# A Perceiver block on one core: Gelu by way of tanh and a polynomial on GpSimd, the temperature MLP spread over three pairs of steps, second scores without a pause

## The reference

```python
scores = qk / math.sqrt(dk)
mean_sim = scores.mean(axis=(-2, -1))
max_sim = scores.max(axis=-1).mean(axis=-1)
probs = jax.nn.softmax(scores, axis=-1)
entropy_proxy = jnp.var(probs, axis=-1, ddof=1).mean(axis=-1)
feats = jnp.stack([mean_sim, max_sim, entropy_proxy], axis=-1)
hidden = jax.nn.gelu(_linear(feats, w1, b1), approximate=False)
hidden = jax.nn.gelu(_linear(hidden, w2, b2), approximate=False)
log_t = jnp.clip(_linear(hidden, w3, b3), LOG_T_MIN, LOG_T_MAX)
t = jnp.exp(log_t)[..., None]
attn = jax.nn.softmax(qk / (2.0 * t), axis=-1)
```

## Time and profile before

| | |
|---|---|
| median of 3 executions | 1214.36 us (1212.34 to 1218.31) |
| profiled execution | span 1213.1 us; its total is not given apart from the span |
| TensorE busy | 1101.5 us (91%) |
| VectorE busy | 812.4 us (67%) |
| ScalarE busy | 765.5 us (63%) |
| GpSimd busy | 406.0 us (33%) |
| mean granted clock of TensorE | 0.897 of 2.4 GHz |
| table loads on ScalarE | 33, 1.283 us each |

### The profile page before, as it was taken

The page is one execution under the profiler, slowest core; times in us unless marked ns, Lnnn a source line. Parts: engine busy times, 40 slices in busy tenths (PEclk is TensorE's granted clock), DMA queues, the critical chain, the costliest instruction groups (busy, mean ns, idle before and its releaser), DMA issues.

```text
span 1213.1 us, 39205 instructions
## 1 busy us (share of the span) xinstructions
PE 1101.5 (91%) x14964; PEld 892.8 (74%) x14964; DVE 812.4 (67%) x2128; ACT 765.5 (63%) x1547; POOL 406.0 (33%) x420
## 2 busy tenths in 40 slices
PE   3867799999999999999999999999999999999864
PEld 3535587878888787878878797878787887867743
DVE  4467667566776776677777776577667777578245
ACT  2434576776766676767766776667767676766521
POOL 2268352223232331433232332333143233331223
PEclk9968798987979897989999898989889898989787
DMA  4610010201010111102010111102020100000000
GB/s 132 193 29 27 23 37 4 61 11 42 19 44 21 36 29 28 37 2 54 11 45 20 37 29 29 36 4 61 2 54 11 45 20 19 3 2 6 8 2 9
DMA packets 46812, 38.85 MB, mean 32 GB/s; under 512 B 14576, under 2 KB 46000, under 8 KB 46640
## 3 DMA queue, kind: packets, MB, share of 16 engines
q1 hardware_dynamic: 46640, 36.41, 11.1%
HBM read 34.30 MB, written 2.10 MB: 30 GB/s over the span
## 4 chain that ended last, share of the span: by engine, by line
PE 75%; DVE 12%; issue 5%; ACT 4%; DMA 2%; POOL 1%; SPq 1%; DVEq 0%; ACTq 0%; POOLq 0%
PE pjp L665 14%; PE s1p L704 14%; PE s2p L735 13%; PE pjp L658 12%; PE pvp L752 8%; DVE est L1392 3%; DVE negm L1386 2%; PE tlp L848 2%; PE tlp L866 1%; PE tlp L787 1%; ACT ering L1045 1%; PE tlp L842 1%; PE s2p L725 1%; PE s2p L645 1%; PE tlp L809 1%
## 5 line engine op out<-in xcount | busy, mean ns | idle before, releaser
L1386 DVE TENSOR_REDUCE negm<-s1p 128x1 f32<-128x400 f32 (+1 forms) x512 | 289.8, 566 | 199.1 <-PE s1p L704 196.6
L1045 ACT ACTIVATE ering<-s1p,negm 128x400 f32<-128x400 f32 (+1 forms) x512 | 303.8, 597 | 118.6 <-DVE negm L1386 112.2
L1056 ACT ACTIVATE pring<-s2p 128x512 f32<-128x512 f32 x427 | 240.8, 565 | 148.1 <-PE s2p L735 145.1
L704 PE MATMUL s1p<-kt,qbd 32*128 32x400 f32 (+1 forms) x1024 | 305.2, 608 | 28.1 <-ACT ering L1045 26.1
L1392 DVE BATCH_NORM_STATS2 est<-ering 128x6 f32<-128x400 f32 (+1 forms) x512 | 290.7, 568 | 19.6 <-ACT ering L1045 19.6
L735 PE MATMUL s2p<-q2bd,kt 32*128 32x128 f32 (+1 forms) x3192 | 244.6, 285 | 0.0
L735 PEld LDWEIGHTS s2p<-q2bd,kt 32*128 32x128 f32 (+1 forms) x3192 | 233.3, 194 | 5.8
L658 PE MATMUL pjp<-cr,wkv 128*128 128x256 f32 (+1 forms) x1344 | 192.4, 295 | 29.7 <-DVE vt L1358 19.2
L1264 POOL TENSOR_TENSOR cr<-stage,cr 128x512 fp32r<-128x512 f32 (+1 forms) x112 | 132.1, 1180 | 234.3 <-ACT cr L1036 234.3
L658 PEld LDWEIGHTS pjp<-cr,wkv 128*128 128x128 f32 x1344 | 171.8, 198 | 45.5 <-issue 29.1
L665 PE MATMUL pjp<-wkv,cr 128*128 128x256 f32 (+1 forms) x1200 | 195.7, 318 | 10.0 <-ACT kt L1018 9.8
(11 more groups left out here) (278 smaller groups left out, 1033.1 us busy)
## 6 DMA issues: line engine op xcount, KB each, us to landing
stage<-in_ctx SPq DMA_DIRECT2D x96, 256.0 KB, 3.0
qbd<-q_dram SPq DMA_DIRECT2D x128, 8.0 KB, 1.8
stage<-in_ctx SPq DMA_DIRECT2D x16, 65.0 KB, 2.5
vt<-in_x SPq DMA_DIRECT2D x1, 1024.0 KB, 6.8
...
```

The source lines that it names most:

```text
L704: nc.tensor.matmul(s1p[u % 3][:, 0:w], qbd[s.par][rows, g, :], kt[s.par][rows, g, lo:lo + w], start=True, stop=True).then_inc(s1_full, 1)
L1045: nc.scalar.activation(ering[:, u % 3, 0:w], s1p[u % 3][:, 0:w], ACT.Exp, bias=negm[s.par][:, p, c:c + 1]).then_inc(s1_exp, 1)
L1056: nc.scalar.activation(ring_place(s, v)[0:m, 0:n], s2_bank(s, v)[0:m, 0:n], ACT.Exp).then_inc(s2_exp, 1)
L1386: nc.vector.tensor_reduce(negm[s.par][:, p, ch:ch + 1], s1p[u % 3][:, 0:w], AX.X, ALU.max, negate=True).then_inc(s1_max, 1)
```

## The change

The Gelu is no longer a ScalarE function. ScalarE computes x/2 and x squared from the matmul's output (`gelu_in`). GpSimd raises a polynomial in x squared to an argument for tanh, in ten operations on 16 or 64 columns, each of which waits for the one before by semaphore. ScalarE computes the tanh (`gelu_tanh`), which is in the table of exp, and GpSimd finishes with two operations. The weights of the MLP are widened with zeros to 128 rows and columns. The three MLP matmuls go to steps 5, 7 and 9, the first ahead of its step's projection and the others behind theirs. Second scores have no pause, projections and context splits move, the last part of the hidden rows' quantization moves from position 68 to 66 (step 4 to 2), and finishing a batch's output from steps 14 and 15 to 12 and 13.

```diff
-PJ_PLAN = [(1, ("k", 4, 0)), (3, ("v", 4, 0)), (5, ("k", 5, 0)), (9, ("v", 5, 0)), (11, ("k", 6, 0)),
-           (12, ("v", 6, 0)), (13, ("m",)), (17, ("k", 0, 1)), (19, ("v", 0, 1)), (21, ("k", 1, 1)), (23, ("v", 1, 1)),
+PJ_PLAN = [(1, ("k", 4, 0)), (3, ("v", 4, 0)), (5, ("k", 5, 0)), (7, ("v", 5, 0)), (9, ("k", 6, 0)),
+           (11, ("v", 6, 0)), (13, ("m",)), (17, ("k", 0, 1)), (19, ("v", 0, 1)), (21, ("k", 1, 1)), (23, ("v", 1, 1)),
...
-CTX_AT = {1: (5, 0), 9: (6, 0), 11: (0, 1), 15: (1, 1), 20: (2, 1), 24: (3, 1), 28: (4, 1)}
+CTX_AT = {1: (5, 0), 4: (6, 0), 11: (0, 1), 15: (1, 1), 20: (2, 1), 24: (3, 1), 28: (4, 1)}
-S2_IDLE = (38, 39)
-S2_AT = [s for s in range(14, 14 + S2U + 2) if s not in S2_IDLE]
-S2_EARLY = S2_AT.index(STEPS + 5)
-STATS_AT = [1, 3, 8, 10]
-MLP_AT = {5: 0, 6: 1, 7: 2}
+S2_AT = list(range(14, 14 + S2U))
+STATS_AT = [1, 3, 9, 11]
+MLP_AT = {5: 0, 7: 1, 9: 2}
-W_AT, GELU_AT, C_AT = 2, 5, 9
-FIN_AT = [14, 15]
+W_AT, C_AT = 2, 10
+GELU_AT = [6, 8]
+FIN_AT = [12, 13]
...
+Q_LAST = T_AT["up1"] + 4
-            T_AT["up1"] + 2: (1, range(0, 2)), T_AT["up1"] + 3: (1, range(2, 4)), 68: (1, range(5, 7))}
+            T_AT["up1"] + 2: (1, range(0, 2)), T_AT["up1"] + 3: (1, range(2, 4)), Q_LAST: (1, range(5, 7))}
-                 68: (1, range(7, 10))}
+                 Q_LAST: (1, range(7, 10))}
...
+                    if MLP_AT.get(step) == 0 and s.has(1, B):
+                        temperature(s, 0)
                     if step in plan:
                         project(s, *plan[step])
-                    if step % 2 == 1 and step in MLP_AT and s.has(1, B):
+                    if MLP_AT.get(step, 0) > 0 and s.has(1, B):
                         temperature(s, MLP_AT[step])
...
-            def gelu(s, n):
+            def gelu_in(s, n):
                 need(act, mlp_full, s.lin(N_MLP, n + 1 - N_MLP))
-                nc.scalar.activation(hid[:, n, :], tlp[0:DH, 0:H], ACT.Gelu,
-                                     bias=col("b1" if n == 0 else "b2", 0, DH)).then_inc(mlp_free, 1)
+                nc.scalar.activation(gx[:, n, :], tlp[:, 0:H], ACT.Identity, bias=halves[:, 6 + n:7 + n],
+                                     scale=0.5).then_inc(ge_in, 1)
+                nc.scalar.activation(gs[:, 0, :], tlp[:, 0:H], ACT.Square,
+                                     bias=col("b1" if n == 0 else "b2")).then_inc(ge_in, 1)
+
+            def gelu_tanh(s, n):
+                need(act, ge, s.lin(2 * GE_N, GE_N * n + GE_N - 1 - 2 * GE_N))
+                nc.scalar.activation(gy[:, n, :], gy[:, n, :], ACT.Tanh).then_inc(ge_th, 1)
...
+                if part == 0:
+                    need(pool, ge_in, s.lin(4, 2 * n + 2 - 4))
+                    step_(0, nc.gpsimd.tensor_tensor(gs[:, 1, :], sq, sq, ALU.mult))
+                    step_(1, nc.gpsimd.tensor_tensor(ga[:, :, :], wide(sq, RQ), erf_r[:, 1, :, :], ALU.mult))
+                    step_(2, nc.gpsimd.tensor_tensor(ga[:, :, :], ga[:, :, :], erf_r[:, 0, :, :], ALU.add))
+                    for k in range(RQ - 1):
+                        top = ga[:, RQ - 1, :] if k == 0 else gb[:, :]
+                        step_(3 + 2 * k, nc.gpsimd.tensor_tensor(gb[:, :], top, gs[:, 1, :], ALU.mult))
+                        step_(4 + 2 * k, nc.gpsimd.tensor_tensor(gb[:, :], gb[:, :], ga[:, RQ - 2 - k, :], ALU.add))
+                    step_(9, nc.gpsimd.tensor_tensor(y, gb[:, :], x, ALU.mult))
+                else:
+                    need(pool, ge_th, s.lin(2, n + 1 - 2))
+                    step_(10, nc.gpsimd.tensor_tensor(y, y, x, ALU.mult))
+                    nc.gpsimd.tensor_tensor(hid[:, n, :], y, x, ALU.add).then_inc(mlp_free, 1)
```

More of the change, by code:

```diff
@@ L886, in slot @@
                             scores2(s, range(at, at + LAST_QUAD))
-                        if step in MLP_AT and s.has(1, B):
-                            temperature(s, MLP_AT[step])
                         s_, v = s.second(step, 2)
@@ L1254, in slot @@
                 for step in range(STEPS):
+                    if s.has(1, B) and step in GELU_AT:
+                        gelu(s, GELU_AT.index(step), 0)
+                    if s.has(1, B) and step - 1 in GELU_AT:
+                        gelu(s, GELU_AT.index(step - 1), 1)
                     s_, at = s.unit(step, 2)
@@ L1297, in last_tile @@
                 rstd_of(2)
-                tail(s.last, 68)
+                tail(s.last, Q_LAST)
                 h_ = blocks16(l_hb[:, 0:FC])
@@ L1687, in last_tile @@
                                                      op1=ALU.subtract), False)
[L1688 removed]
+                tail(s.last, Q_LAST, s)
                 dve.wait_ge(lp, LP["out"])
```

62 lines of the change are left out of this document (45 added, 17 removed).

## The result

The changed kernel takes 1321.65 us (median of 4 runs, 1319.09 to 1324.43) where the kernel before takes 1214.34 on the same chip: ratio 1.084, 95% interval 1.080 to 1.089. I had 1243 us, and 1266 as the upper end. The direction was right, the size was not: +107 us in place of +29. Some executions of a kernel run over 1.5% longer than its fastest, at a lower granted clock (e7's of 1336 us, e8's of 1271 and 1274, one of before of 1230), and all ratios leave these out.

The account below looks back on a forecast made before the run. TensorE, busy 91% of 1213.1 us and partly at its lower clock, was taken as the bound. Terms +36 (slots like 9), -10 (like 8) and +3 (slot 16) gave +29, 1243 us; range 1196 to 1266.

Parts of the forecast that it names:

- Slots like slot 8, to step 14: Nine slots without tail quantization in steps 0 to 4: pause moved, not removed; -1.1 us each, -10 us in all.
- Slots like slot 9, to step 14: Six slots quantizing a tail tile: late statistics leave TensorE idle 5.9 us; +6 us each, +36 in all.
- four held operations: Slots like slot 9: two-input VectorE statistics (lines 1421, 1423, 1428, 1429) each wait for one GpSimd operation.
- that rule: VectorE also contends with GpSimd in a 2-port mode, delaying quantization operations 5 and 6: 0.8 us more per slot, six slots.
- The second scores close up: Second scores move from steps 8 to 11 to 6 to 9: same instructions, in the cover already counted.
- With the low clock again behind the longer pause: Slots like slot 8: low clock for 6.8 us from about 605, so step 14 starts at 613.2, not 610.4.
- The removal: Table switches go; the pause and slow clock behind it, 4 to 6 us, could be won in a slot like slot 8.
- The clock didn't hold: Rival: the clock stays at 2.4 GHz behind the 2.4 us pause in slots like slot 8; 1195 us, chance 0.22.
- GpSimd did hold VectorE up: Against the rival that GpSimd hardly holds VectorE up, +2 us in six slots; 1219 us, chance 0.18.
- Short GpSimd operations at 0.4 us: Rival: each Gelu takes 1.3 us longer, about +1.9 us a slot, +28 in 15 slots; 1271 us, chance 0.08.
- the wait of 2 us or more before the third matmul: Sign: in all slots the third MLP matmul waits 2 us or more for GpSimd.

Follow-up runs that it names:

- e7: e5 with the Gelu's chain on GpSimd, computing all of the reference; 1319.61 us, ratio 1.076 to the kernel before.
- e8: e5 with the Gelu's polynomial and product on VectorE in place of tanh alone; 1250.5 us, ratio 1.025 to the kernel before.
- e9: e6 with the first MLP matmul ahead of the projection of step 5; 1246.72 us, ratio 1.022 to the kernel before.
- e3: The changed kernel without the GpSimd chain, ScalarE computing tanh alone (not the reference's values); 1288.42 us, ratio 1.056 to the kernel before.
- e1: The changed kernel with the last piece of the quantization back in step 4; 1321.08 us, ratio 1.082 to the kernel before.
- e6: e5 with second scores, projections, last context part and finish in the changed kernel's order; 1244.95 us, ratio 1.019 to the kernel before.
- e5: e4 with the MLP widened and its matmuls in steps 5, 7 and 9, otherwise the old order; 1195.53 us, ratio 0.977 to the kernel before.
- e2: The changed kernel with the old order of second scores, projections, last context part and finish; 1318.0 us, ratio 1.079 to the kernel before.
- e4: The kernel before with Tanh in place of Gelu on ScalarE, so no table switch (not the reference's values); 1179.22 us, ratio 0.966.
- e14: e12 with six more large unread matmuls at the end of step 12; 1213.68 us, ratio 0.995 to the kernel before.
- e11: e8 with a shorter, coarser Gelu form, two VectorE operations ahead of the tanh; 1239.84 us, ratio 1.017 to the kernel before.
- e12: The kernel before with nine large unread matmuls in the pause at the end of step 7, in 14 slots; 1207.01 us, ratio 0.992.

## Why the prediction was right in direction and short in size

The steps of the prediction, in its order, with what the runs gave. Parts are of 1218 us.

**Slots like slot 8, to step 14: right.** -0.8 us against -1.1. The third matmul could start 10.4 us behind the first (641.43 - 630.99), as I had it (606.0 - 595.44 = 10.6), so the chain was priced right; GpSimd's operations took 0.22 and 0.32 us and followed at 0.08. The pause was 1.27 us and not 2.4, since TensorE came later: I had left the second scores of step 8 out of its cover, with which that step's scores take 1.56 us and not 0.9. Part of the agreement is luck: the clock fell 1.9 us later in the slot than I had it, and then didn't come back before step 14, where I had it back 1.4 us ahead of it.

**Slots like slot 9, to step 14: near.** I had the wait at 5.9 us, and it is 6.42 to 6.50; step 14 came 7.2 us later, and the sum had +6. Without the chain the move of the quantization is worth 3.4%, 41 us (e9 to e3); I had +36 for it and the chain together. With the chain in place, taking it back gives 0.3% (e1), within the intervals. I named four held operations; two of them (lines 1483 and 1490) were held, and in place of the other two it was line 1494's two, which I had left out. That the number of held operations came out the same is luck. Line 495, with one input, took 1.57 us beside the context subtraction (it ended 0.37 us behind it), and 0.51 in e8 (there line 496) without one. The Trainium skill (GPSIMD Engine Reference, Specifications) says that VectorE contends with GpSimd in a 2-port mode too. The trace of line 495 agrees, if its mode is one, which no run shows; the measured wait lies between the 5.9 us without that rule and the 6.7 with it.

**The second scores close up: this step failed.** The prediction says of them "the same instructions, in the cover above", a price of nothing. Measured without the chain, by e6 against e5, it is 4.2%, 51 us, the largest term of all; with the chain in place it is 0.5% (e2), since the old order then leaves the chain without its cover. The instructions are the same, but moved into steps 6 to 9, and the whole value projection from step 9 to 7, they leave steps 9 to 14 with small matmuls only. In the same way "With the low clock again behind the longer pause, for the 6.8 us of the earlier trace rows" took the length of a low stretch from one slot of another order. It was 20.5 us, and in slot 9 10.2, 6.8 and 6.8, where before had 6.8 in all (windows of 0.5 us, added up). And I ended each slot's account at step 14, as if nothing behind it could differ: 6.0 us in slot 8 and 5.4 in slot 9 lie behind that line. Nine and six of these are 86 us, and with the +29 of my sum that makes +115, against +107 measured. Not every slot is like the two that were read: from its first MLP matmul to the next slot's, each of slots 1 to 3 lost only 2.0 to 3.7 us, where slot 8's reading gives 5.2.

**The spread of the MLP**, which I didn't cost apart from its waits, is 1.1% (e4 to e5), the widened weights included. It carries small matmuls into steps 7 and 9, and the low clock rose from 215 to 251 us; which of the two costs the time isn't shown.

**The shift row** (16.1 us of waits before step 14's second scores, new) I hadn't named. It stays at 11.6 us in e6 and is 0.5 in e5, so it comes with the new order. Probably TensorE, without second scores in steps 10 to 13, gets there ahead of ScalarE's row; no run tests this. Of the 49.4 us by which e6's execution is longer than e5's, all idle time, this wait among it, makes 6.7, and the same matmuls at the lower clock 42.7.

**The removal** had no term of its own in my sum, only 4 to 6 us as what could be won in a slot like slot 8. The table switch alone is worth 3.4%, 42 us (e4), or 2.6 us in each of 16 slots. The chain gave 2.9% of the time back (e3 to after). Built up: -3.4 + 1.1 + 4.2 + 0.3 + 3.4 + 2.9 = +8.4% (the parts are rounded), the measured ratio, as it must be, since each run starts from the one before. The split holds in this order of steps alone: e7 shows the chain at 10% where the new order doesn't cover it, and e2 the order at 0.5% where the chain is in place.

**The rivals.** The clock didn't hold. GpSimd did hold VectorE up. Short GpSimd operations at 0.4 us fell: they took 0.22. Of my signs, the wait of 2 us or more before the third matmul didn't come either (0.9 to 1.9 us). The case that came, a low clock that lasts through thin steps, was none of mine, though the earlier trace rows had a busy engine at 0.50 for all 6.80 us, and I read that as an echo of the pause.

Open: why e14's extra matmuls at step 12 didn't pay, why a low stretch lasts as long as it does (27.3 us in a slot of e11), and which of the new order's lists does most of its harm. As the clock shifts with every edit, a difference of 1% between two runs doesn't price the edit alone. A kernel that keeps the exact Gelu and the 1179 us of e4 wasn't found; the fastest that computes the whole reference is e12, 0.8% below before.
